# A transformer layer on one core: the second layer norm's rows centred by ScalarE, its scale moved into the FP4 block scales

## The reference

```python
x = x + attn(layernorm(x))          # X is 8 x 2048 x 256, no learned scale or shift
x = x + ffn(layernorm(x))
# attn: Q = xpos(x WQ), K = xpos(x WK), V = x WV; softmax(Q K^T) * 0.9**|n-m|, then @ V
# ffn:  fp4_linear(silu(fp4_linear(x, w_gate)) * fp4_linear(x, w_up), w_down), inner width 704
def _layernorm(x, eps=1e-05):
    return (x - mean) / sqrt(var + eps)
def fp4_quant_dequant(x):           # on the rows and on the weights, blocks of 16 columns
    scale = maximum(max(abs(xb)) / 6.0, 1e-12)
    xn = xb / scale                 # then to the nearest of 0, .5, 1, 1.5, 2, 3, 4, 6, times scale
```

## Time and profile before

| what | us |
|---|---|
| median of 3 runs | 2724.89 (2723.97 to 2725.95) |
| the profiled execution's own time | 2723.85 |
| its span, first to last instruction | 2722.0 |
| PE busy in the span | 2621.2 (96%) |
| DVE busy | 2211.8 (81%) |
| POOL busy | 1780.4 (65%) |
| ACT busy | 1465.1 (54%) |

### The profile page before, as it was taken

The page is one execution under the profiler, slowest core; times in us unless marked ns, Lnnn a source line. Parts: engine busy times, 40 slices in busy tenths (PEclk is TensorE's granted clock), DMA queues, the critical chain, the costliest instruction groups (busy, mean ns, idle before and its releaser), DMA issues.

```text
span 2722.0 us, 52226 instructions
## 1 busy us (share of the span) xinstructions
PE 2621.2 (96%) x16418; PEld 2353.1 (86%) x16418; DVE 2211.8 (81%) x4969; ACT 1465.1 (54%) x2815; POOL 1780.4 (65%) x1563
## 2 busy tenths in 40 slices
PE   7998899999999999999999999999999999999996
PEld 7887778988899889988998899888998899889996
DVE  7999877788878887788778887888778878888885
ACT  6665545455545555555455555555545555555553
POOL 6989946666665666566665666666666666576664
PEclk9999999999999999999999999999999999999998
DMA  7776410012000300021002200120003100310000
GB/s 291 289 266 233 164 42 19 24 44 91 24 24 20 115 24 24 18 102 39 24 19 73 69 20 22 40 100 22 23 21 108 31 24 21 101 38 24 19 24 16
DMA packets 135884, 183.51 MB, mean 67 GB/s; under 512 B 10064, under 2 KB 93136, under 8 KB 135632
## 3 DMA queue, kind: packets, MB, share of 16 engines
q1 hardware_dynamic: 135632, 180.33, 19.3%
HBM read 102.69 MB, written 77.59 MB: 66 GB/s over the span
## 4 chain that ended last, share of the span: by engine, by line
PE 68%; POOL 9%; issue 4%; ACT 3%; DVE 2%; POOLq 0%; ACTq 0%; DVEq 0%
PE score L406 21%; PE acc L525 16%; PE ring L406 15%; PE acc L406 8%; PE ring L498 4%; PE ring L543 3%; POOL probs L831 3%; POOL vals L816 2%; ACT probs L693 2%; POOL h_buf L852 2%; POOL hq_buf L856 1%; DVE smax L1042 1%; DVE xqT L1029 1%; POOL xv L837 1%; PE ring L490 1%
## 5 line engine op out<-in xcount | busy, mean ns | idle before, releaser
L831 POOL TENSOR_TENSOR probs<-probs,decay 128x512 f32<-128x512 f32 (+3 forms) x432 | 526.1, 1233 | 389.2 <-ACT probs L693 389.2
L406 PE MATMUL score<-keys,q_st 128*128 128x512 f32 x3072 | 767.8, 399 | 2.6 <-ACT probs L693 1.9
L406 PEld LDWEIGHTS score<-keys,q_st 128*128 128x128 f32 x3072 | 561.9, 189 | 116.0 <-issue 2.1
L525 PE MATMUL acc<-vals,pT 128*128 128x256 f32 x4416 | 594.1, 286 | 9.6 <-DVE pT L1029 9.6
L525 PEld LDWEIGHTS acc<-vals,pT 128*128 128x128 f32 x4416 | 556.1, 190 | 24.1 <-issue 9.2
L406 PE MATMUL ring<-w_gu,xqT 128*128 128x512 f32 (+1 forms) x2304 | 510.2, 375 | 0.0
L406 PEld LDWEIGHTS ring<-w_gu,xqT 128*128 128x128 f32 x2304 | 419.3, 188 | 63.6
L663 ACT ACTIVATE pT<-ring 128x512 fp32r<-128x512 f32 (+3 forms) x432 | 226.9, 535 | 449.6 <-PE ring L498 442.1
L1042 DVE TENSOR_REDUCE smax<-score 128x1 f32<-128x1024 f32 x256 | 312.9, 1222 | 165.5 <-PE score L406 164.6
L837 POOL TENSOR_TENSOR xv<-xv,xe 128x256 f32<-128x256 f32 x128 | 94.0, 734 | 435.9 <-DVE xv L910 435.9
L1029 DVE TENSOR_TENSOR pT<-ring,pT 128x512 fp32r<-128x512 f32 (+3 forms) x432 | 251.0, 606 | 72.2 <-ACT pT L663 72.1
(11 more groups left out here) (120 smaller groups left out, 4067.9 us busy)
## 6 DMA issues: line engine op xcount, KB each, us to landing
k_dram<-keys SPq DMA_DIRECT2D x56, 512.0 KB, 4.2
keys<-k_dram SPq DMA_DIRECT2D x56, 512.0 KB, 7.3
q_raw<-q_dram SPq DMA_DIRECT2D x129, 128.0 KB, 2.6
x_in<-X SPq DMA_DIRECT2D x32, 512.0 KB, 4.0
q_dram<-q_stage SPq DMA_DIRECT2D x32, 512.0 KB, 5.1
x_res<-X SPq DMA_DIRECT2D x128, 128.0 KB, 2.0
out<-x_res SPq DMA_DIRECT2D x128, 128.0 KB, 1.7
v_dram<-v_stage SPq DMA_DIRECT2D x28, 512.0 KB, 2.9
```

What stands on the lines that cost most here:

```text
L406: mm = pe.matmul(dst, stat(a, k), mov(m, k), start=i == 0, stop=i == n - 1)
L525: mm = pe.matmul(pv_out, pT[g % 2][:, a, j * P:(j + 1) * P], vals[m][:, kb, :], start=i == 0, stop=i == n - 1)
L831: pool.tensor_tensor(probs[:, k0 * P:k1 * P], probs[:, k0 * P:k1 * P], decay[:, off:off + (k1 - k0) * P], ALU.mult).then_inc(decayed, 1)
```

## The change

The centring leaves DVE: ACT writes mean - x (the row with its sign turned) into `xv`, between the first and the second piece of its silu. DVE takes the block maxima of that, so the maxima no longer wait for POOL's power. The variance is multiplied by 36 before the power, so POOL's result is a sixth of the scale (`rstd6`). It enters `xs` in the place of the constant 1/6. POOL then makes `rstd2` with a product by six, and DVE multiplies by it in the product that was L1111, now with three operands. The turned sign is taken up by the gate and up weights, which are stored with the opposite sign.

```diff
 # DVE, residual
-                then(dve.bn_aggr(mv2[:], st2[:]))
-                wait()
-                dve.tensor_scalar(var2[:], mv2[:, 1:2], EPS, None, ALU.add).then_inc(ln2_var, 1)
+                dve.bn_aggr(mv2[:], st2[:]).then_inc(ln2_mean, 1)
+                dve.wait_ge(ln2_mean, g + 1)
+                dve.tensor_scalar(var2[:], mv2[:, 1:2], EPS, 36.0, ALU.add, ALU.mult).then_inc(ln2_var, 1)
 # DVE, x_scales
-                dve.wait_ge(ln2_rstd, g + 1)
+                meanwhile(0)
+                dve.wait_ge(x_centred, g + 1)
+                then(dve.tensor_reduce(xam[:], blocks(xv[:]), AX.X, ALU.max, apply_absolute_value=True))
+                meanwhile(1)
+                dve.wait_ge(ln2_sixth, g + 1)
                 if has(at, t - 1):
                     dve.wait_ge(xq_ready, g)
-                then(dve.tensor_scalar(xv[:], x_res[:, t % XR, :], mv2[:, 0:1], rstd2[:, 0:1], ALU.subtract, ALU.mult))
-                meanwhile(0)
                 wait()
-                then(dve.tensor_reduce(xam[:], blocks(xv[:]), AX.X, ALU.max, apply_absolute_value=True))
-                meanwhile(1)
+                then(dve.tensor_scalar(xs[:], xam[:], rstd6[:, 0:1], 1e-12, ALU.mult, ALU.max))
                 wait()
-                scales(then, wait, xam[:], xs[:], xrs[:])
+                then(dve.reciprocal(xrs[:], xs[:]))
 # DVE, x_levels
-                then(dve.tensor_tensor(blocks(xv[:]), blocks(xv[:]), spread(xrs[:], XB), ALU.mult))
+                dve.wait_ge(ln2_rstd, tile(at, t) + 1)
+                then(dve.scalar_tensor_tensor(blocks(xv[:]), blocks(xv[:]), rstd2[:, 0:1], spread(xrs[:], XB), ALU.mult, ALU.mult))
 # ACT: gate(at, s - 2, lambda: x_centred_rows(at, s - 1)) calls this before piece 1 (at once, if there is no gate)
+            def x_centred_rows(at, t):
+                if has(at, t):
+                    g = tile(at, t)
+                    act.wait_ge(ln2_mean, g + 1)
+                    if has(at, t - 1):
+                        act.wait_ge(xq_ready, g)
+                    act.activation(xv[:], x_res[:, t % XR, :], ACT.Identity, bias=mv2[:, 0:1], scale=-1.0).then_inc(x_centred, 1)
 # POOL, rstd_tile
-                    pool.wait_ge(ln2_var, tile(at, t) + 1)
-                    pool.tensor_tensor(rstd2[:], var2[:], minus_half[:, 0:1], ALU.pow).then_inc(ln2_rstd, 1)
+                    g = tile(at, t)
+                    pool.wait_ge(ln2_var, g + 1)
+                    pool.tensor_tensor(rstd6[:], var2[:], minus_half[:, 0:1], ALU.pow).then_inc(ln2_sixth, 1)
+                    pool.wait_ge(ln2_sixth, g + 1)
+                    pool.tensor_tensor(rstd2[:], rstd6[:], six[:], ALU.mult).then_inc(ln2_rstd, 1)
 # once per kernel: a third constant, and the sign of the gate and up weights (w_sign is -1 for them, 1 for the down weights)
+            pool.memset(six[:], 6.0).then_inc(constants_set, 1)
-op = act.activation(dst(0), w_view(...), ACT.Copy)
+op = act.activation(dst(0), w_view(...), ACT.Copy, scale=w_sign(i))
-op = dve.tensor_tensor(dst(1), w_view(...), dst(0).bitcast(F32), ALU.subtract)
+op = dve.scalar_tensor_tensor(dst(1), w_view(...), w_sign(i), dst(0).bitcast(F32), ALU.mult, ALU.subtract)
```

More of the change, by code:

```diff
@@ L135, in build @@
         st1, mv1, var1, rstd1 = sb("st1", [P, CT, 6]), *([sb(f"{n}{i}", w) for i in range(2)] for n, w in (("mv1", [P, CT, 2]), ("var1", [P, CT]), ("rstd1", [P, CT])))
-        st2, mv2, var2, rstd2 = sb("st2", [P, 6]), sb("mv2", [P, 2]), sb("var2", [P, 1]), sb("rstd2", [P, 1])
+        st2, mv2, var2, rstd2, rstd6 = sb("st2", [P, 6]), sb("mv2", [P, 2]), sb("var2", [P, 1]), sb("rstd2", [P, 1]), sb("rstd6", [P, 1])
         aggr_pad = sb("aggr_pad", [P, 1])
-        minus_half = sb("minus_half", [P, CT])
+        minus_half, six = sb("minus_half", [P, CT]), sb("six", [P, 1])
         smax, nmax = sb("smax", [P, 2]), sb("nmax", [P, 2])
@@ L198, in build @@
         pv_done, dn_done, x1_done, y_done = sem("pv_done"), sem("dn_done"), sem("x1_done"), sem("y_done")
-        ln2_step, ln2_var, ln2_rstd = sem("ln2_step"), sem("ln2_var"), sem("ln2_rstd")
+        ln2_step, ln2_mean, ln2_var, ln2_sixth, ln2_rstd, x_centred = sem("ln2_step"), sem("ln2_mean"), sem("ln2_var"), sem("ln2_sixth"), sem("ln2_rstd"), sem("x_centred")
         xq_step, xg_ready, xq_ready = sem("xq_step"), sem("xg_ready"), sem("xq_ready")
@@ L202, in build @@
         hq_step, hv_ready, hg_ready, hq_ready = sem("hq_step"), sem("hv_ready"), sem("hg_ready"), sem("hq_ready")
-        NSTEP_W, NSTEP_LN2, NSTEP_XQ, NSTEP_HQ = 6, 3, 7, 5
+        NSTEP_W, NSTEP_LN2, NSTEP_XQ, NSTEP_HQ = 6, 2, 6, 5
         def later(j):
@@ L264, in w_jobs, with w_sign @@
             return moves, [(0, P, 0, 2 * P, lambda x: w_gu[x][:, :, to(2):to(2) + P]), (0, P, 2 * P, P, lambda x: w_gu[x][:, :, to(2) + P:to(2) + P + P // 2])]
+        def w_sign(i):
+            return -1.0 if i // W_SLOTS < 2 else 1.0
         def w_view(ap, dst):
@@ L589, in _ @@
         def _(act):
-            act.wait_ge(constants_set, 2)
+            act.wait_ge(constants_set, 3)
             act.activation(exp_ready[:], zero[:], ACT.Exp)
@@ L667, in weights @@
                 for p0, p1, col, n, dst in w_jobs(i)[1]:
-                    op = act.activation(dst(0), w_view(bank(at, "w", i)[p0:p1, col:col + n], dst(0)), ACT.Copy)
+                    op = act.activation(dst(0), w_view(bank(at, "w", i)[p0:p1, col:col + n], dst(0)), ACT.Copy, scale=w_sign(i))
                 op.then_inc(hi_done, 1)
@@ L698, in exponentials, with gate @@
                                bias=psum_row[:, s % 2, 1:2]).then_inc(summed, 1)
-            def gate(at, t):
+            def x_centred_rows(at, t):
                 if has(at, t):
+                    g = tile(at, t)
[3 more added lines that the diff above has]
+                    act.activation(xv[:], x_res[:, t % XR, :], ACT.Identity, bias=mv2[:, 0:1], scale=-1.0).then_inc(x_centred, 1)
+            def gate(at, t, meanwhile):
+                if not has(at, t):
+                    meanwhile()
+                else:
                     for p, (p0, w) in enumerate(PIECES):
+                        if p == 1:
+                            meanwhile()
                         if p == 0 and has(at, t - 2):
@@ L730, in step @@
                     values(at, c)
-                gate(at, s - 2)
+                gate(at, s - 2, lambda: x_centred_rows(at, s - 1))
             for x in v_out:
@@ L748, in _ @@
             pool.memset(zero[:], 0.0).then_inc(constants_set, 1)
-            pool.wait_ge(constants_set, 2)
+            pool.memset(six[:], 6.0).then_inc(constants_set, 1)
+            pool.wait_ge(constants_set, 3)
             def rstd_chunk(i, c):
@@ L1033, in weights_lower @@
                 for p0, p1, col, n, dst in w_jobs(i)[1]:
-                    op = dve.tensor_tensor(dst(1), w_view(bank(at, "w", i)[p0:p1, col:col + n], dst(1)), dst(0).bitcast(F32), ALU.subtract)
+                    op = dve.scalar_tensor_tensor(dst(1), w_view(bank(at, "w", i)[p0:p1, col:col + n], dst(1)), w_sign(i), dst(0).bitcast(F32), ALU.mult, ALU.subtract)
                 op.then_inc(freed, 1)
```

## The result

The changed kernel takes 2708.81 us in the median of 4 runs (2708.02 to 2710.07), the kernel before 2725.26 in 4 runs: a ratio of 0.994 with a 95% interval of 0.9926 to 0.9955. That is 0.6% or 16.5 us faster, outside the range given (2720.0 to 2731.5). The profiled execution took 2708.02 us, 15.83 less than that of before.

What follows compares the result with a forecast made beforehand. PE bounds the kernel except some 5.8 us per batch. Seven batches -0.8, fill -0.9 and end -0.3 make -2.0 us: 2721.9 from the profiled 2723.85, or 2723 as median; range 2720 to 2731.5.

Steps and rivals of the forecast that it cites:

- Once per kernel: Setup before the loop: weight copies keep shape and count, the third constant is one small memset; claimed to cost nothing.
- for what I haven't seen: Remainder of the chances, 5%, left for causes that neither the forecast nor any rival named.
- The bound: Tile phase: PE sets the pace, except for some 5.8 us per batch, mostly waits for POOL's L856 in steps 0 to 2.
- The chain of the norm: POOL's power to L856 in steps 0 to 2, followed to L1111's end; the change was to move that end.
- d: Delay of POOL's later pieces by its added product and wait: 0.35 us, with 0.30 and 0.73 as ends.
- Steps 1 and 2: Each batch: L898's successor gets in before the values, the final product ends 0.28 behind them; gain 0.23 us each.
- Step 0: Start of each batch: ACT's silu is late, both DVE holds follow L816 and end d later; loss 0.35 us.
- The fill: First steps of the kernel: the product ends earlier, gaining 0.86 us of PE's 1.56 us wait; summed as -0.9.
- The rival of the reloads: ACT reloads its tables around the centring in each tile: +14 us in all, about 2737; 4%.
- The unheld product: POOL does not hold DVE's three-operand product, so L856 comes up to 2 us earlier: 2698 us; 5%.
- The dear product: POOL's product by six costs as much as the power, 0.55 us: +6.0 us, 2731; 10%.
- The missed gap: L898's successor misses its place between L831's piece and L816 in steps 1 and 2: 2731, or 2727; 10%.

Runs made afterwards that it cites:

- e1: The kernel before with two unused 128x1 tensors where the change allocates its new ones, so later tensors move by 64 bytes; no instruction differs: 2714.97 us, ratio 0.9963.
- e2: The change with its two new columns in the padding of existing tensors, so that no tensor moves against the kernel before: 2719.79 us, ratio 0.9982.
- e7: e2 without POOL's product by six, DVE multiplying by `rstd6` instead, so rows come out smaller by a factor of six: 2723.18 us, ratio 0.9998.
- e9: e8 with POOL's copies of the values, except values(0), moved to the end of its steps 0, 1 and 2: 2711.94 us, ratio 0.9953.
- e8: The change with two more unused 128x1 tensors ahead of `w_gu`, so the weight products' operands are also 64 bytes further apart: 2703.45 us, ratio 0.9923.

## Why the prediction was wrong

*The step that failed* is "Once per kernel": "The weight copies keep shape and count, and the third constant is one small memset while the first rows are loaded: nothing, as their length stays." It counted what the new lines execute and not what they allocate. `rstd6` and `six` move every later tensor by 64 bytes against the keys and values, and that alone gives 10 us (e1), some 60% of the result. No rival covered it, and the 5% "for what I haven't seen" was too little for a kernel whose PE is busy for 96% of the span: 1% in the pace of its matmuls is 26 us, more than anything that the waits can give.

*The bound* was read rightly. PE sets the pace in 13 of 16 steps, the 5.8 us of a batch lie in steps 0 to 2, and DVE's fall by 32 us of busy time, against the 171 of L1094, gained nothing in the other steps.

*The chain of the norm* was right, and its sum of -2.0 too small; e2 measured -5.0. With 2719.79 us e2 lies just outside the range (2720.0) too: the second term that was mis-sized is d, taken as 0.35 with 0.30 as its lower end. Term by term:

- d, POOL's delay, is 0.25 us, not 0.35. The product takes 0.19 (0.17 forecast), but it starts 0.08 behind the power's end where 0.15 was taken from L837 and L841, and the next piece starts 0.05 before the product's end.
- The product of three operands is held and ends 0.27 behind the values (0.28 forecast). The Trainium skill (SBUF — State Buffer, Who interferes with whom) says that a DVE instruction with two SBUF inputs contends with a GpSimd one that reads SBUF. The trace agrees: the same product takes 0.47 to 0.48 us where POOL is idle (e7, e9) and 2.1 to 2.2 beside the values.
- Steps 1 and 2 gain 0.37 each: 0.58 from the end of the product less 0.25, and 0.04 since the copy of the values ran 2.42 instead of 2.46. The forecast had 0.23. Step 0 loses 0.19 (0.35 forecast). Per batch -0.55 instead of -0.11, in seven batches -3.9 instead of -0.8.
- The fill: PE's wait for the second tile's product fell from 1.56 to 0.61 us, 0.95 for the 0.86 forecast. A second wait there, for hq_buf at 410 us, fell from 0.88 to 0.17, which the prediction didn't have: the fill gave -1.95 against -0.9 (-1.9 in e2, so this is the norm and not the place). At the end PE's last wait of this kind fell from 1.37 to 1.11, the 0.3 forecast.
- The centring on ACT takes 507 ns, with as many table loads as before (128 and 128). The rival of the reloads did not occur. The Trainium skill (ScalarE: Activation LUTs, Table sets: the hidden batching unit) says that cheap functions such as identity are in every table set. The trace agrees: an Identity between two silus loads nothing.
- PE waits 1.10 us for `pT` in step 0 where it waited 0.87: +0.23, the direction and about the size of d.
- These terms add up to 6.1 us, where e2's runs gave 5.0; the interval of its ratio, 0.9973 to 0.9991, is 2.5 to 7.4 us.

One reading of the prediction is too wide: "DVE instructions that read only from SBUF are thus held until the POOL instruction ends." Beside the same L816 of step 0 the block maxima (L1097, from 930.50) took 0.41 us and the reciprocal (L900, from 932.18) 0.25, as they do elsewhere. L1094, L898 and L1111 are held, not every such instruction; the sum used only the holds of these three and their successors.

*The rivals.* The unheld product is excluded by L1134's 2.12 us. The dear product is excluded by its 0.19. The missed gap, given 10%, is not in the change's profile, where the successor of L898 takes 0.23 to 0.35 us in steps 1 and 2 of all seven batches. It occurs in e7 in all of these steps, and in step 1 of two batches of e8 (2.29 and 2.27 us) and one of e2 (2.21), each time behind one of the longer falls of the clock. Its condition was put as "0.36 us late"; a quarter of a microsecond in POOL's start is enough.

Still open: why the distance of two operands changes the pace of a matmul by 2 to 3 ns in 130, why 32, 64, 96 and 128 bytes act as they do, and why the score product gained 6.5 us in e8. No run here has varied one distance in small steps with the rest held.

## What to carry to other kernels

In a kernel that PE bounds, compare the mean time of each group of matmuls before and after an edit, even one that touches no matmul: a new tensor of one column moves what is made after it, and here that was worth twice the edit itself. Compare in stretches at the same granted clock, since falls of the clock alone put 2.1 us on the sum of one group here (`vals,pT` in e2). To judge an edit alone, hold the places (put the column into padding that is there), and run the kernel before with unused tensors of the same size. Where DVE and POOL exclude each other, count for each DVE instruction whether it is issued before or behind the next POOL instruction; an instruction more on POOL can gain time, and a long one on POOL is best put where DVE has nothing that PE waits for.

## What the runs showed of the hardware

- The pace of fp32r matmuls of 128x128 by 128x256 changes when the loaded operand moves in SBUF against the streaming one: 4416 of them took 584 to 586 us with the distance 64 or 96 bytes longer, and 593 to 597 with it unchanged or 32 or 128 bytes longer; in one batch at full clock 72.5 to 72.8 us against 73.5 to 74.2. Moving all tensors by the same 64 bytes changed nothing (593.8).
- DVE's three-operand product on 128x256, both large inputs in SBUF, that starts 0.5 to 0.6 us behind the start of POOL's copy of the values runs 2.1 to 2.2 us instead of 0.47 and ends 0.28 behind it, in all 21 cases of the change's profile.
- DVE's scaling of 128x16 (0.23 us) is held as well: 2.2 to 2.3 us where its record starts 0.12 to 0.24 behind the copy's, and 2.46 where it starts 0.03 ahead of it (e7, step 2). It took 0.23 to 0.36 where it starts 0.12 or more ahead.
- POOL's product on 128x1 takes 0.19 us where its power takes 0.55, and the wait between the two costs 0.08.
